# The order of work within an attention round: maximum products, values and relative products dealt out anew

## The chip, the cores and the metric

The kernel is one launch on one core of a Trainium2 chip. It computes one whole transformer layer. The metric is the device time in microseconds (us) of that launch. The engines are named PE (TensorE, matrix products), DVE (VectorE), ACT (ScalarE), POOL (GpSimd) and SP (which only issues DMA transfers). Each engine runs its own list of instructions in order, and they wait for one another by semaphores.

## The reference

Everything is float32, batch 2, sequence 2048, width 256, 16 heads of 16, relative positions clipped at 64.

```
x = x + attention(layernorm(x));  x = x + ffn(layernorm(x))

q, k, v = split(x @ W_qkv + b_qkv);  q = q / sqrt(16)
score = q . k  +  q . pe_k[clip(j - i, -64, 64) + 64]
attn  = softmax(score)
ctx   = attn @ v  +  sum_j attn[i, j] * pe_v[clip(j - i, -64, 64) + 64]
out   = ctx @ W_out + b_out

ffn: fp4_linear(silu(fp4_linear(x, w_gate)) * fp4_linear(x, w_up), w_down)
     (fp4: both operands rounded in blocks of 16 to a grid of 8 magnitudes)
```

## The kernel before, in words

The program has three parts, one after the other: `projections` (layer norm, Q, K, V), `attention`, and `ffn`. The change is in `attention` alone.

**Rounds.** Attention runs in 32 rounds. A round is one block of 512 queries of one group of four heads (2 batches x 4 groups x 4 blocks). The keys of a batch (2048) are walked in 16 steps, so a round has 16 steps, and each step has four half units: two tiles' worth of scores, 128 keys by 512 queries each, called **S** here. PE computes the scores transposed (keys in the partitions) into one of four PSUM banks `psS`, and ACT takes the exponential out of the bank. Steps 0 and 1 are the band near the diagonal (`near_half`, lines 916 and 923: four transposes that add the relative scores, then four products). Steps 2 to 15 are far from it (`far_half`, line 934).

**The maximum comes first.** The exponential needs the maximum of each row, and it is found one round ahead. For that PE computes the same scores once more, queries in the partitions, 64 products of 128 x 512 a round. Such a **maximum product** (**M** in the tables, line 826) goes to one of three PSUM banks `psA`, and DVE reduces it to one column (line 1115, `take`). The three banks go round: product number j waits until DVE has read product number j - 3 (`slot_free`). Three more things use that ring of banks, once a round each: the turned context (**D**, line 864), the denominators turned back (**B**, line 873), and the relative value products (**P**, line 959).

**The other letters.** **V** is the values of a step (line 848, `far_values`): probabilities times V, accumulated in the bank `psC`; a step's V is issued in the step after it, and in step 2 the letter stands for the band's values (line 946). **R** is the relative products (line 836): q times the table of relative keys, for the next round, into two banks of `psS`, from which ACT copies them to `rel_scores` (line 1061) and DVE later takes their maximum (`rel_maxima`, line 1120). There are four R in a round. After the last of them a DMA writes `rel_scores` to DRAM and two DMAs read it back skewed as `rel_near` for the next round. **T** (line 856) turns the negated maxima, and **F** (line 971) adds the relative values to `psC`. In steps 7 to 12 of the middle rounds, DVE also does one small operation a step on the weights of the FFN (lines 1207 to 1234).

**What sets the order.** The order is written out by hand: `ORDER` has one word of letters per step. PE goes through a word and issues what each letter says. DVE goes through the same words and does what concerns it, in the same order. ACT goes through its units in order. `RATE` counts the M of each step. The M of steps 13 to 15 (`AHEAD`) belong already to the round after the next, since the next round's maxima are made final at the start of step 13. `place`, `rel_place` and `half_at` number the half units and the relative products in the one sequence of `psS` banks. `RSTEP = 4` says that the four R stand at the end of steps 4 to 7.

## Time and profile before

| | |
|---|---|
| median of 3 runs | 2372.92 us (2371.45 to 2374.48) |
| profiled execution | 2376.86 us |
| its span, from first to last instruction | 2375.1 us |
| PE busy / DVE busy / ACT busy | 2254.8 / 1884.2 / 1431.0 us |
| attention's 32 rounds | from 173.9 us to about 1970 us of the span |
| mean granted TensorE clock | 0.976 of full speed |

A busy PE in this profile is not a PE at its peak: a product's record lasts 0.38 us, while the next one starts 0.22 us after it, so the records overlap and short waits hide under them. What PE really loses is read from the starts: where two successive products start further apart than the same pair does elsewhere, PE has waited.

### The profile page before, as it was taken

To read this page: it belongs to the slowest core of one execution; us is meant where nothing else is said; L and a number is where in the kernel's file an instruction comes from. 1 tells how busy PE (TensorE), PEld (TensorE's weight loads), DVE (VectorE), ACT (ScalarE), POOL (GpSimd) and SP (SyncE) were. 2 spreads that over 40 slices of the span, in tenths; PEclk is the share of its full clock that TensorE was granted. 3 is DMA by queue.
4 is the path that set the end of the run, shared out by engine and by line. 5 is a ranking of instruction groups with operands and counts; after the bars stand their busy time and mean duration, and the time that the engine had idled before them with its cause. 6 is when DMAs were issued, how large, how long until landed. Compare 5 with 4: busy or idle time off the path is not lost. (4 is left out here: it accounts for less than half of the span.)

```text
span 2375.1 us, 53033 instructions
## 1 busy us (share of the span) xinstructions
PE 2254.8 (95%) x21292; PEld 1157.4 (49%) x21292; DVE 1884.2 (79%) x3617; ACT 1431.0 (60%) x2720; POOL 600.4 (25%) x355
## 2 busy tenths in 40 slices
PE   6989999999999999999999999999999997999997
PEld 3514444444444444444444444444444444666665
DVE  5787788888888788878887888878888725999997
ACT  3406666677776666666666666666777673444442
POOL 5502222333322222222222222323332220111111
PEclk9959999999999999999999999999999998999999
DMA  5733533332334234433332342333222221111110
GB/s 160 195 90 92 134 90 93 97 93 84 92 100 116 83 98 106 110 88 93 93 97 79 103 97 84 97 92 93 84 84 84 83 72 43 45 44 44 47 50 20
DMA packets 275682, 210.68 MB, mean 89 GB/s; under 512 B 17058, under 2 KB 266628, under 8 KB 275332
## 3 DMA queue, kind: packets, MB, share of 16 engines
q1 hardware_dynamic: 274308, 203.37, 31.2%
q0 software_dynamic: 1152, 4.19, 0.6%
q8 instruction: 159, 2.61, 0.5%
q14 instruction: 63, 0.52, 0.1%
HBM read 113.35 MB, written 93.34 MB: 87 GB/s over the span
## 5 line engine op out<-in xcount | busy, mean ns | idle before, releaser
L1115 DVE TENSOR_REDUCE amax<-psA 128x1 f32<-128x512 f32 x2048 | 1300.8, 683 | 271.6 <-PE psA L826 267.2
L1082 ACT ACTIVATE probs<-psS 128x512 f32<-128x512 f32 x1792 | 928.7, 610 | 372.1 <-PE psS L934 370.2
L826 PE MATMUL psA<-keys,queries 96*128 96x512 bf16 x2048 | 782.0, 392 | 23.1 <-DVE amax L1115 17.9
L934 PE MATMUL psS<-queries,keys 102*128 102x512 bf16 (+7 forms) x2176 | 642.7, 343 | 2.1 <-issue 2.0
L848 PE MATMUL psC<-probs,vals 128*32 128x512 f32 (+7 forms) x4352 | 481.0, 528 | 4.2 <-issue 3.7
L784 POOL TENSOR_TENSOR band_probs<-band_probs,side 128x2048 f32<-128x2048 f32 x64 | 289.0, 4537 | 506.8 <-PE psC L946 506.8
L826 PEld LDWEIGHTS psA<-keys,queries 96*128 96x128 bf16 x2048 | 197.2, 98 | 444.2 <-DVE amax L1115 316.0
L934 PEld LDWEIGHTS psS<-queries,keys 102*128 102x128 bf16 (+1 forms) x2176 | 208.0, 98 | 186.2 <-ACT rel_scores L1061 18.1
L1077 ACT ACTIVATE band_probs<-psS 128x512 f32<-128x512 f32 x256 | 153.0, 598 | 159.6 <-PE psS L923 159.5
L848 PEld LDWEIGHTS psC<-probs,vals 128*32 128x32 f32 (+1 forms) x4352 | 89.4, 102 | 197.0 <-ACT probs L1082 128.5
L1438 PE MATMUL psG<-w_gate_up_T,f_xqT 128*128 128x352 f32 x512 | 160.4, 467 | 0.9 <-ACT f_xqT L1492 0.9
L1061 ACT COPY rel_scores<-psS 128x512 f32<-128x512 f32 x256 | 137.2, 590 | 31.1 <-PE psS L836 30.7
L916 PE MATMUL psS<-ident,rel_near 128*128 128x128 f32 x1024 | 155.5, 274 | 0.0
L790 POOL TENSOR_TENSOR band_probs<-band_probs 128x2048 f32<-128x2048 f32 x32 | 145.2, 4538 | 6.0 <-POOL band_probs L788 3.2
L916 PEld LDWEIGHTS psS<-ident,rel_near 128*128 128x128 f32 x1024 | 129.1, 142 | 23.6 <-issue 0.9
L1377 POOL TENSOR_TENSOR f_hq<-f_h_grid,f_h_scale 128x704 f32<-128x704 f32 x32 | 44.4, 1387 | 375.0 <-DVE f_h_grid L1606 375.0
L1438 PEld LDWEIGHTS psG<-w_gate_up_T,f_xqT 128*128 128x128 f32 x512 | 96.5, 193 | 50.5 <-issue 3.0
L770 POOL CAST shift<-shift_res 32x128 bf16<-32x128 f32 x32 | 9.0, 281 | 423.4 <-ACT shift_res L1050 423.4
L923 PE MATMUL psS<-queries,keys 102*128 102x128 bf16 (+1 forms) x1024 | 100.2, 220 | 4.9 <-DMA queries<-shift 4.9
L764 POOL MEMSET rel_near<- 128x256 f32 x16 | 5.1, 317 | 380.5 <-DMA rel_near<-rel_skew 380.5
L1470 PE MATMUL psD<-w_down_T,f_hqT 128*128 128x256 f32 (+1 forms) x384 | 96.2, 393 | 2.0 <-ACT f_hqT L1498 2.0
L1492 ACT COPY f_xqT<-psH 128x256 f32<-128x256 f32 x32 | 11.9, 373 | 129.1 <-PE psH L1429 129.1
(161 smaller groups left out, 2017.3 us busy)
## 6 DMA issues: line engine op xcount, KB each, us to landing
rel_skew<-rel_scores SPq DMA_DIRECT2D x32, 2048.0 KB, 9.2
rel_near<-rel_skew SPq DMA_DIRECT2D x64, 1024.0 KB, 8.2
keys<-k_ring SPq DMA_DIRECT2D x48, 256.0 KB, 5.8
queries<-q_parts SPq DMA_DIRECT2D x192, 64.0 KB, 2.4
ctx_d<-rden SPq DMA_DIRECT2D x32, 256.0 KB, 2.3
ctx_in<-ctx_d SPq DMA_DIRECT2D x32, 256.0 KB, 2.7
q_parts<-parts SPq DMA_DIRECT2D x16, 384.0 KB, 3.0
k_ring<-parts SPq DMA_DIRECT2D x12, 384.0 KB, 3.1
```

The source lines that it names most:

```text
L784: p.tensor_mul(both, both, c.side[:, e, None, :].broadcast_to([P, APAIRS, P])).then_inc(side_cut, 1)
L790: p.tensor_add(band[:, 0].rearrange("p h u q -> p (h u q)"), band[:, 0].rearrange("p h u q -> p (h u q)"), band[:, 1].rearrange("p h u q - ...
L826: t.matmul(small("M", m, n), qs[0:NR, qb, h, u * P:(u + 1) * P], keys[0:NR, par, h, c0:c0 + NQ], start=True, stop=True).then_inc(small_rea ...
L848: ins = t.matmul(psC[32 * h:32 * h + v.shape[1], q0:q0 + k], v, probs[:, n % 4, h % 2, o:o + k], start=False, stop=False, skip_group_check ...
L916: t.matmul(bank[:, u * P:(u + 1) * P], near[:, h * CH + u, e, :], c.ident[:], start=(u == 0), stop=False, is_transpose=True, skip_group_ch ...
L923: ins = t.matmul(bank[:, u * P:(u + 1) * P], keys[0:nr, par, h, c0:c0 + P], qs[0:nr, qb, h, u * P:(u + 1) * P], start=False, stop=(u == CH ...
L934: ins = t.matmul(bank[:, o:o + k], keys[0:nr, par, h, c0:c0 + P], qs[0:nr, qb, h, q0:q0 + k], start=True, stop=True, skip_group_check=True)
L1061: a.copy(rel[:, x:x + 2, :].rearrange("p x r -> p (x r)"), psS[:, j % SBANKS, :]).then_inc(unit_done, 1)
L1077: ins = a.activation(band[:, e, 2 * c2 + half].rearrange("p u q -> p (u q)"), src, ACT.Exp)
L1082: ins = a.activation(probs[:, n % 4, half], src, ACT.Exp)
L1115: v.reduce_max(amax[:, pair, k:k + 1], small("M", m, n), AX.X).then_inc(small_taken, 1)
L1438: ins = t.matmul(psG[:, half, 0:GU], xqT[:, k, cc, :], wgu[:, cc, half * GU:(half + 1) * GU], start=(cc == 0), stop=(cc == 1))
```

## The change

The words of `ORDER` are written anew. A round still has 64 M, 64 S, 14 V and the band's values, 4 R, and one each of D, B, P, F and T. What changes is where they stand:

- The M of the 16 steps were 7 6 5 4 3 3 3 4 4 4 5 4 3 3 3 3. They are now 9 4 5 4 6 1 3 4 5 2 4 5 0 4 5 3. The last three steps have 12 instead of 9, so 12 products (before: 9) are done ahead of the first round.
- V stood near the end of its step, behind the fourth S in most steps. It now stands in mid-step, mostly behind the second or third S.
- The four R stood at the end of steps 4, 5, 6 and 7. They now stand in steps 0, 1, 4 and 6.
- The maximum of the relative products had no letter: it stood behind the third M of the step after its R. It now has the letter **X**, in steps 1, 2, 5 and 7.

```diff
-RSTEP = 4
 RUNITS = APAIRS // 4
 SEQ = UNITS + RUNITS
+RSTEPS = (0, 1, 4, 6)
 ORDER = (
-    "SMSMVMSMSMMM", "SMSMMSDMSMM", "SMSMMVBSMSM", "SMSMSMSVM",
-    "SMSSMSVRM", "SMSSMSVRM", "SMSSMSVRM", "SMSMSMSVRM",
-    "SMSMSMSVPM", "SMSMSMSVM", "SMSMSMSMVFM", "SMSMSMSVM",
-    "SMSSMSVM", "SMSSMSVMT", "SMSSMSVM", "SMSSMSVM",
+    "SMMSMVMMMSMSRMM", "SMSMXSMSMDR", "MSSMXMVBSMMS", "SSMSMVMSM",
+    "SMSSMSMVMMRM", "SSMXSVS", "MSMSSSMVR", "MSMMXSVSMS",
+    "MSSMSMVPMSM", "SSMSVMS", "SSMSMMVFMS", "MSMSVSMSMM",
+    "SSSVS", "SMSSMSMVMT", "MSMVMSMSMS", "MSSSMVMS",
 )
...
-    return n if ends else n + min(max(n // 2 - RSTEP, 0), RUNITS)
+    return n if ends else n + sum(r < n // 2 for r in RSTEPS)
...
-    return 2 * (RSTEP + k) + 2 + k
+    return 2 * RSTEPS[k] + 2 + k
...
-                                rel_products(it + 1, qb1, step - RSTEP)
+                                rel_products(it + 1, qb1, RSTEPS.index(step))
...
-                    if n % 2 == 1 and RSTEP <= n // 2 < RSTEP + RUNITS and not ends:
-                        copy_rel(it + 1, n // 2 - RSTEP)
+                    if n % 2 == 1 and n // 2 in RSTEPS and not ends:
+                        copy_rel(it + 1, RSTEPS.index(n // 2))
...
-                    k = 0
                     for kind in ORDER[step]:
                         if kind == "M":
                             if todo:
                                 take(*todo.pop(0))
-                            k += 1
-                            if RSTEP < step <= RSTEP + RUNITS and k == 3 and not ends:
-                                rel_maxima(it + 1, step - RSTEP - 1)
+                        elif kind == "X" and not ends:
+                            rel_maxima(it + 1, RSTEPS.index(step - 1))
```

Three places show what moves. The first is PE in the second round, from the last products of step 1 to the band's values in step 2 (`psA` is the ring of the maximum products, `psS` holds scores or relative products, `psC` the values). Before:

```order
L916 MATMUL psS<-ident,rel_near 128x128 x4
L923 MATMUL psS<-queries,keys 128x128 x4
L826 MATMUL psA<-keys,queries 128x512 x2
L934 MATMUL psS<-queries,keys 128x384
L934 MATMUL psS<-queries,keys 128x128
L826 MATMUL psA<-keys,queries 128x512
L934 MATMUL psS<-queries,keys 128x384
L934 MATMUL psS<-queries,keys 128x128
L826 MATMUL psA<-keys,queries 128x512 x2
L946 MATMUL psC<-band_probs,vals 32x128 x4
```

And now, from the last maximum product of step 1 on:

```order
L826 MATMUL psA<-keys,queries 128x512
L864 MATMUL psA<-ident,ctx_sum 128x128 x4
L836 MATMUL psS<-rel_rows,queries 128x256 x4
L826 MATMUL psA<-keys,queries 128x512
L934 MATMUL psS<-queries,keys 128x384
L934 MATMUL psS<-queries,keys 128x128
L934 MATMUL psS<-queries,keys 128x384
L934 MATMUL psS<-queries,keys 128x128
L826 MATMUL psA<-keys,queries 128x512 x2
L946 MATMUL psC<-band_probs,vals 32x128 x4
```

Between the last near half of step 1 and the band's values there were five maximum products; now there are three, and the relative products and the turned context stand among them.

The second place is PE from the end of step 7 (the products behind the relative products or behind the third S) to the relative value products in step 8. Before:

```order
L836 MATMUL psS<-rel_rows,queries 128x256 x4
L826 MATMUL psA<-keys,queries 128x512
L934 MATMUL psS<-queries,keys 128x512
L826 MATMUL psA<-keys,queries 128x512
L934 MATMUL psS<-queries,keys 128x512
L826 MATMUL psA<-keys,queries 128x512
L934 MATMUL psS<-queries,keys 128x512
L826 MATMUL psA<-keys,queries 128x512
L934 MATMUL psS<-queries,keys 128x512
L848 MATMUL psC<-probs,vals 32x512 x4
L959 MATMUL psA<-band_probs,tv 32x32 x64
```

And now:

```order
L848 MATMUL psC<-probs,vals 32x512 x4
L934 MATMUL psS<-queries,keys 128x512
L826 MATMUL psA<-keys,queries 128x512
L934 MATMUL psS<-queries,keys 128x512
L826 MATMUL psA<-keys,queries 128x512
L934 MATMUL psS<-queries,keys 128x512 x2
L826 MATMUL psA<-keys,queries 128x512
L934 MATMUL psS<-queries,keys 128x512
L826 MATMUL psA<-keys,queries 128x512
L848 MATMUL psC<-probs,vals 32x512 x4
L959 MATMUL psA<-band_probs,tv 32x32 x64
```

The strict alternation of M and S is broken by a pair of S, and the V of step 7 stands before the last two S of that step instead of behind them.

The third place is DVE in a round of the middle, from step 6 to step 10 (`amax` is the maximum of one product, `rel_max_of` that of relative products, the `w_` tiles are the FFN's weights). Before:

```order
L1115 TENSOR_REDUCE amax<-psA 128x1 x3
L1120 TENSOR_REDUCE rel_max_of<-rel_scores 128x4
L1115 TENSOR_REDUCE amax<-psA 128x1
L1210 TENSOR_SCALAR w_scale<-w_scale 128x16
L1115 TENSOR_REDUCE amax<-psA 128x1 x3
L1120 TENSOR_REDUCE rel_max_of<-rel_scores 128x4
L1155 TENSOR_TENSOR rel_products<-psA,mask_q 128x16x16x2
L1115 TENSOR_REDUCE amax<-psA 128x1
L1213 RECIPROCAL w_scale<-w_scale 128x16
L1115 TENSOR_REDUCE amax<-psA 128x1 x4
L1216 TENSOR_SCALAR w_scale<-w_scale 128x16
L1115 TENSOR_REDUCE amax<-psA 128x1 x5
```

And now (the line numbers of the new kernel are two higher here, except those of the weights):

```order
L1117 TENSOR_REDUCE amax<-psA 128x1 x3
L1122 TENSOR_REDUCE rel_max_of<-rel_scores 128x4
L1117 TENSOR_REDUCE amax<-psA 128x1
L1210 TENSOR_SCALAR w_scale<-w_scale 128x16
L1117 TENSOR_REDUCE amax<-psA 128x1 x3
L1157 TENSOR_TENSOR rel_products<-psA,mask_q 128x16x16x2
L1117 TENSOR_REDUCE amax<-psA 128x1 x2
L1213 RECIPROCAL w_scale<-w_scale 128x16
L1117 TENSOR_REDUCE amax<-psA 128x1 x2
L1216 TENSOR_SCALAR w_scale<-w_scale 128x16
L1117 TENSOR_REDUCE amax<-psA 128x1 x4
```

One maximum of relative products has left step 8, and the M of the steps 9 and 10 have become fewer.

## Rows read from the trace of the kernel before

**Rows 1.** The page: busy times, and 40 slices with PE's share and granted clock.
```profile
PE 2254.8 (95%) x21292; PEld 1157.4 (49%) x21292; DVE 1884.2 (79%) x3617; ACT 1431.0 (60%) x2720; POOL 600.4 (25%) x355
...
PE   6989999999999999999999999999999997999997
...
PEclk9959999999999999999999999999999998999999
```

**Rows 2.** Windows of an undisturbed, a disturbed and the last-but-one round; columns in line one.
```profile
core 0: us, PE busy (x) PEld busy (x) DVE busy (x) ACT busy (x) POOL busy (x), PEclk, DMA share, GB/s
...
679.00:734.40 55.40, 55.03 (x611) 26.55 (x610) 45.49 (x80) 38.34 (x74) 14.96 (x7) 1.00 0.37 99
734.40:793.90 59.50, 56.37 (x611) 26.61 (x610) 45.78 (x80) 38.53 (x74) 15.29 (x8) 0.97 0.35 92
...
1866.80:1919.90 53.10, 52.89 (x602) 25.48 (x600) 39.27 (x66) 37.58 (x74) 15.23 (x8) 1.00 0.30 86
```

**Rows 3.** Timeline of PE, step 2: start, duration, line, what, [idle before].
```profile
688.25 0.60 PE L826 MATMUL psA<-keys,queries 96*128 96x512 bf16 x2
...
689.12 0.38 PE L934 MATMUL psS<-queries,keys 99*128 99x384 bf16 x2
689.41 0.39 PE L826 MATMUL psA<-keys,queries 96*128 96x512 bf16 x1
690.01 0.39 PE L826 MATMUL psA<-keys,queries 96*128 96x512 bf16 x1 [0.21 <-DVE amax L1115]
```

**Rows 4.** Timeline of PE, end of step 8 of the same round.
```profile
710.06 0.38 PE L826 MATMUL psA<-keys,queries 96*128 96x512 bf16 x1
710.28 0.38 PE L934 MATMUL psS<-queries,keys 102*128 102x512 bf16 x1
710.75 0.39 PE L826 MATMUL psA<-keys,queries 96*128 96x512 bf16 x1
710.97 0.38 PE L934 MATMUL psS<-queries,keys 102*128 102x512 bf16 x1
711.28 1.06 PE L848 MATMUL psC<-probs,vals 128*32 128x512 f32 x8
712.16 1.40 PE L959 MATMUL psA<-band_probs,tv 128*32 128x32 f32 x128
713.50 0.39 PE L826 MATMUL psA<-keys,queries 96*128 96x512 bf16 x1
```

**Rows 5.** Timeline of DVE, steps 2 and 8 to 9 of that round.
```profile
688.66 3.08 DVE L1115 TENSOR_REDUCE amax<-psA 128x1 f32<-128x512 f32 x5 [0.19 <-PE psA L826]
...
709.41 0.68 DVE L1120 TENSOR_REDUCE rel_max_of<-rel_scores 128x4 f32<-128x512 f32 x1
710.01 0.68 DVE L1115 TENSOR_REDUCE amax<-psA 128x1 f32<-128x512 f32 x1
710.61 0.16 DVE L1216 TENSOR_SCALAR w_scale<-w_scale 128x16 f32<-128x16 f32 x1
710.68 1.88 DVE L1115 TENSOR_REDUCE amax<-psA 128x1 f32<-128x512 f32 x3
...
714.84 0.42 DVE L1219 TENSOR_TENSOR w_tmp<-w_rows,w_scale 128x256 f32<-128x256 f32 x1
715.17 2.48 DVE L1115 TENSOR_REDUCE amax<-psA 128x1 f32<-128x512 f32 x4
```

**Rows 6.** Timeline of ACT, steps 6 and 7 of that round.
```profile
705.94 1.07 ACT L1061 COPY rel_scores<-psS 128x512 f32<-128x512 f32 x2
706.90 2.08 ACT L1082 ACTIVATE probs<-psS 128x512 f32<-128x512 f32 x4
```

**Rows 7.** Timeline of PE in the disturbed round, first product after the gap.
```profile
773.19 0.39 PE L826 MATMUL psA<-keys,queries 96*128 96x512 bf16 x1 [2.60 <-issue]
```

**Rows 8.** All waits of the span: engine, line, waited for: total us, times, longest.
```profile
PEld psA L826 <- DVE amax L1115: 316.0, 584, 2.1
```

**Rows 9.** Timeline of DVE ahead of the first round.
```profile
130.67 38.35 DVE L1115 TENSOR_REDUCE amax<-psA 128x1 f32<-128x512 f32 x64
...
169.59 5.47 DVE L1115 TENSOR_REDUCE amax<-psA 128x1 f32<-128x512 f32 x9
```

More of the change, by code:

```diff
@@ L1000, in iteration @@
                                 turn_maxima(it + 1)
+                        elif kind != "V":
+                            continue
                         elif step == 0:
```

## The prediction, written before the changed kernel ran

> **What bounds the kernel now.** I read the page first, then windows of single rounds, then the timelines of PE, DVE and ACT within one round. The page puts PE at 95% of the span with DVE at 79% behind it, and PE's share is 9 tenths or more in nearly every slice of attention [rows 1]. That is not yet a proof, since PE's records overlap. The windows show the size of a round: 55.40 us undisturbed, with DVE busy for 45.49 and ACT for 38.34 of them, and the clock at its full 2.4 GHz [rows 2]. So DVE and ACT each have 10 us or more to spare, and the round is PE's own work plus what PE waits for.
>
> How much it waits is in the starts. A maximum product (M) and a score half (S) follow each other at 0.22 us (710.06, 710.28) [rows 4]. In step 2 one M starts 0.60 us after the one before it (689.41, 690.01) and an earlier one 0.29 after its S [rows 3]. At the end of step 8 one starts 0.47 us behind its S (710.28, 710.75) [rows 4]. Against the 0.22 expected, that is 0.38, 0.07 and 0.25 us lost. I read the same six places (two in step 2, one each in steps 3, 8, 9 and 10) in the 29 rounds that begin between 233.0 and 1808.4 us. In the 23 undisturbed ones they sum to 1.16 to 1.73 us, mean 1.40; the round without them is 54.0 to 54.4 us, mean 54.2. In six rounds in which PE has a gap of 1.5 to 3.9 us with nothing to wait for, like the one of 2.60 us [rows 7], they sum to 1.09: DVE catches up during the gap. No other place of the round loses over 0.05 us on average.
>
> All six are M waiting for a bank that DVE has not yet emptied; that pair leads the waits of PE's loads, 584 times [rows 8].
>
> **The rule of these waits, from rows.** DVE starts on a product 0.41 us after PE starts it (688.25, 688.66), and then takes one each 0.60 us: five in 3.08, the last of 0.68 [rows 3, 5]. PE may start the product three later some 0.07 us after DVE is done: the second of those five begins at 689.26, ends at 689.94, and PE starts at 690.01. So product j can start 0.41 + 0.68 + 0.07 = 1.16 us after the start of product j-3, if DVE had no backlog. M and S in strict turns put four M into 1.31 us: the fourth has 0.15 us to spare, and each further one 0.16 less, because DVE needs 0.60 where PE brings one each 0.44. The fifth is on time by a hair; the sixth is late. Whatever else DVE does there adds to it: a maximum of relative products 0.60 (709.41 to 710.01), a weight operation 0.07 to 0.33 (710.61 to 710.68; 714.84 to 715.17) [rows 5], a mean of 0.24 over its ten kinds.
>
> **Step by step, before.** PE's time of a step (0.22 for M and S, 0.66 for a near S, 1.00 and 0.09 more for V, 0.45 for R, 1.33 for P, as their starts show) against DVE's: steps 7 to 11 take PE 3.27, 4.03, 2.82, 3.91, 2.82 us and DVE 3.23, 3.84, 2.64, 3.24, 2.64. For five steps DVE has next to no slack, so what it owes after step 7 comes due at the last M of steps 8, 9 and 10. In step 2 five M stand within 1.4 us behind an already full DVE. The same account puts the last M of step 8 at 0.40 late, those of step 9 at 0.21 and step 10 at 0.42, and those of step 2 at 0.45 in all; read: 0.44, 0.15, 0.27 and 0.46. It is good to about 0.15.
>
> **The change part by part.** No product, exponential or reduction is added or removed, so the 54.2 us stay and only waits can move.
>
> *The M dealt out anew.* PE's and DVE's time of the 16 steps, in us: 6.13/5.40, 4.41/3.16, 4.81/4.20, 2.82/2.40, 3.71/3.60, 2.17/1.19, 3.05/1.80, 2.82/3.23, 4.25/3.84, 2.39/1.44, 3.69/2.64, 3.04/3.24, 1.95/0.24, 2.94/3.07, 3.04/3.00, 2.61/1.80. Where DVE has more (7, 11, 13) the step before or behind has 1 us or more to spare (6, 12, 15), and the three banks carry the excess. I went through every M with the rule above. No product comes late. The least to spare is 0.15 us, at the fourth of four M in strict turns (into step 15), then 0.16 in step 0 and 0.18 to 0.20 once each in steps 2, 3 and 4. With each weight operation at 0.33 instead of 0.24, still none is late. So the six waits go: 1.40 us of a round.
>
> *V in mid-step.* It is the wait that this change could add: V of a step needs all four exponentials of that step, and it now stands two or three S into the next instead of four. ACT takes one each 0.49 us (four in 2.08) and a relative copy likewise [rows 6]; a bank is full 0.42 us after its S starts and the exponential lasts 0.60, so V can start 1.08 us after the last S of its step if ACT has no backlog. Before, V had 0.9 us or more to spare everywhere. Now it is 0.10 in step 11 (M S M S V behind the last S), 0.23 in step 15, 0.28 in step 12, 0.32 in steps 3 and 9, 0.49 and 0.54 in 8 and 10, more elsewhere. None late: cost 0. Queued behind a late V would be the next S and M, thus both other engines. V waiting for ACT doesn't occur in this trace; the bounds are 0 and what the second rival works out.
>
> *R in steps 0, 1, 4, 6.* 0.45 us on PE and 0.97 on ACT each, wherever they stand. Steps 0 and 1 are where ACT is idle most, since a near half takes PE 0.66 us plus its M. The banks that they take are free in time (least to spare 0.2 us, for an S in step 15). Their maxima (X) find the copy finished: the closest is step 2, where the copy ends 0.6 us before DVE gets there. The last R ends a step earlier, so the DMA out and back starts 3 us earlier and stays hidden. POOL's work on the band needs some 14 us between steps 2 and 8, of which there are 19. T still stands in step 13; steps 14 and 15 behind it are 0.4 us longer, which helps the shift's way back.
>
> *Twelve products ahead instead of nine.* Before the first round they run at DVE's pace, 38.35 / 64 = 0.60 us [rows 9]: 1.8 us more. The last-but-one round has three fewer, at 0.22: 0.65 us less, of 53.10 [rows 2].
>
> **The sum.** 23 x 1.40 + 6 x 1.09 = 38.7; the first and the last-but-one round, with fewer operations on DVE, about 1 each: 2.0; less 1.8, plus 0.65: 39.6. I take 1 off for places that are free by less than 0.2 us only on average: 38.6. From the profiled execution, 2376.9 - 38.6 = 2338.3 us; that execution lies 3.9 above the median of the runs, so the median becomes 2334. The rest of the span (projections, FFN) doesn't change.
>
> **Two rules of the Trainium skill.** The round's clock is 1.00 in spite of its waits of up to 0.4 us, and 0.97 in a round with the 2.60 us gap [rows 2, 7]. The Trainium skill ("TensorE: Matmul & The Clock Gate", section on a second HAM failure mode) says that short idles from cycling through PSUM banks make the clock swing. The trace disagrees here: there is no swing to be won back. By that rule the six dips would go as well, and 0.03 of 59.5 us, six times, would be 11 us more.
>
> PE's loads are busy for 26.55 of 55.40 us, DVE for 45.49 [rows 2]. The Trainium skill ("Perfetto Trace Analysis", on identifying the most-contended engine) counts TensorE by its weight loads and takes the busiest engine as the bound, so DVE. This is the third rival below.
>
> **The rivals.** *Half comes back* (12%). The spared times of 0.15 to 0.2 us are about as small as the account's own error. If every place with under 0.2 is late by 0.1 on average, and the backlog carries on, some 0.7 us a round return: 31 x 0.7 = 22, so 2356 us. For it: the account was off by 0.15 in step 10. Against: there it called too much, not too little.
>
> *V waits for ACT* (4%), the side on which it gets slower. If ACT's end reaches a V later than the 0.06 us I used, the spared times run out one by one. At 0.7 us more, the seven V named above are late by 0.60, 0.47, 0.42, 0.38, 0.38, 0.21, 0.16: 2.6 us a round against 1.4 saved, so 30 x 1.2 = 36 slower, 2409 us. It decides from about 0.5 us on. Against: DVE's end reaches PE in 0.07.
>
> *DVE is the bound* (4%). Then a round is DVE's 45.49 us and its own waits, reordering brings none of it away, and it stays at 2373. Against: DVE idles for 9.9 us a round and PE never for more than 0.4.
>
> **How the numbers follow.** The forecast has 80%, its own range 2325 to 2342 (the account's error of 0.15 us at one or two places a round, and PE's six gaps, 1.5 to 3.9 us each, which may be one or two more or fewer). The low end below, 2322, adds some other small waits that vanish. The high end, 2352, takes in most of the first rival. A change within 0.2% (4.7 us, about what a measurement of this kernel can tell) is 4%, slower 4%, faster 92%.
>
> **What would show it.** Right: rounds of 54.0 to 54.4 us instead of 55.4, no M starting over 0.3 us behind its predecessor outside the gaps, the waits of PE's loads for DVE well under 316 us, a first round that starts 1.8 us later. Wrong: undisturbed rounds of 55 us and more; V starting later than 0.31 us behind its predecessor in steps 11, 12 and 15 with ACT named as releaser; or new late M in steps 4, 7, 8 or 15.

## The result, and the profile after

| | before | after |
|---|---|---|
| median | 2372.61 us (2371.45 to 2374.48, 4 runs) | 2345.88 us (2339.8 to 2347.76, 4 runs) |
| profiled execution, its span | 2376.86, 2375.1 us | 2346.05, 2344.3 us |
| attention's first round begins, its last begins | 173.9, 1919.9 us | 175.5, 1886.3 us |

The ratio is 0.9882, with a 95% interval of 0.9863 to 0.9901: faster by 27 us, 1.2%, where 38.6 were forecast. The time lies in the forecast's range, but above the likeliest case's own range (2325 to 2342).

The page after, the rows that answer to [rows 1]:

```profile
PE 2235.5 (95%) x21292; PEld 1168.8 (50%) x21292; DVE 1905.2 (81%) x3617; ACT 1435.7 (61%) x2720; POOL 600.7 (26%) x355
...
PE   6989999999999999999999999999999996999997
...
PEclk9959999999999999999999999999999998999998
```

DVE has the same 3617 instructions and is busy for 21 us more. So some operations now last longer: that is the first trace of what the forecast missed.

Windows of three rounds and of seven microseconds after, in the columns of [rows 2]: a usual round, one with a gap, the last-but-one, and the stretch around the gap.

```profile
675.33:729.42 54.09, 54.09 (x611) 26.86 (x609) 45.58 (x81) 38.46 (x74) 14.96 (x7) 1.00 0.38 101
729.42:790.12 60.70, 57.22 (x611) 27.15 (x609) 46.72 (x81) 38.79 (x74) 15.28 (x8) 0.94 0.34 91
...
1833.79:1886.26 52.47, 52.04 (x598) 25.55 (x597) 37.51 (x63) 38.00 (x74) 15.29 (x8) 1.00 0.30 87
...
764.00:771.00 7.00, 3.62 (x12) 0.64 (x12) 2.11 (x4) 1.99 (x4) 0.00 (x0) 0.71 0.53 149
```

The usual round fell from 55.40 to 54.09 us, as predicted. The one with the gap did not fall: 59.50 before, 60.70 now, with a clock of 0.94 instead of 0.97.

PE in step 2 after, the answer to [rows 3]:

```profile
686.10 0.60 PE L934 MATMUL psS<-queries,keys 99*128 99x384 bf16 x4
686.54 0.60 PE L826 MATMUL psA<-keys,queries 96*128 96x512 bf16 x2
687.07 1.96 PE L946 MATMUL psC<-band_probs,vals 128*32 128x128 f32 x64
```

The 0.60 us between two M is gone; they form one row of two at 0.22. The waits of PE's loads for DVE, the answer to [rows 8], fell by 126 us:

```profile
DVE amax L1117 <- PE psA L826: 201.7, 430, 4.6
PEld psA L826 <- DVE amax L1117: 190.0, 299, 2.3
```

**Where the 30.8 us of the span went.** The 23 shortest of the 29 middle rounds, called undisturbed here, give 23 x (55.58 - 54.26) = 30.3. The six longest, those with the larger gaps, give 4.4 (355.5 to 351.1), the last-but-one 0.6, the first nothing (59.05 to 59.15). Ahead of the first round 1.6 are lost, and 2.8 behind the start of the last one. Two things stand out. In 7 of the 23 rounds one M in step 8 still comes 0.38 to 0.69 us late, 0.15 in the mean over all 23; this is most of why their mean is 54.26 and not 54.1. And eight rounds have gaps of 0.5 to 3.5 us (14.8 in all), where six (13.6) had them before. They are not quite the same rounds: the 19th after the first had a gap of 3.85 us before and has 0.56 now (61.61 to 54.71 us), while the fifth had none and has 1.95 now (55.48 to 57.88).

### The profile page after: what moved, and what is told of

The parts are those of the page before. It is cut to its first block and busy times, and to the rows that moved or that the text cites. A ratio compares the mean times of both kernels' runs of the same rounds, so it can differ in the third digit from the quotient of the medians.

```text
span 2344.3 us, 53033 instructions
## 1 busy us (share of the span) xinstructions
PE 2235.5 (95%) x21292; PEld 1168.8 (50%) x21292; DVE 1905.2 (81%) x3617; ACT 1435.7 (61%) x2720; POOL 600.7 (26%) x355
## 3 DMA queue, kind: packets, MB, share of 16 engines
q1 hardware_dynamic: 274308, 203.37, 31.4%
## 5 line engine op out<-in xcount | busy, mean ns | idle before, releaser
L826 PE MATMUL psA<-keys,queries 96*128 96x512 bf16 x2048 | 747.9, 391 | 6.2 <-DVE amax L1117 5.6
L934 PE MATMUL psS<-queries,keys 102*128 102x512 bf16 (+7 forms) x2176 | 596.2, 344 | 7.4 <-issue 6.9
L826 PEld LDWEIGHTS psA<-keys,queries 96*128 96x128 bf16 x2048 | 191.7, 98 | 319.5 <-DVE amax L1117 190.0
L934 PEld LDWEIGHTS psS<-queries,keys 102*128 102x128 bf16 (+1 forms) x2176 | 202.6, 98 | 270.1 <-ACT probs L1084 100.0
L1122 DVE TENSOR_REDUCE rel_max_of<-rel_scores 128x4 f32<-128x512 f32 x128 | 86.3, 675 | 2.3 <-ACT rel_scores L1063 2.3
```

The costliest lines, as they stand in the source:

```text
L826: t.matmul(small("M", m, n), qs[0:NR, qb, h, u * P:(u + 1) * P], keys[0:NR, par, h, c0:c0 + NQ], start=True, stop=True).then_inc(small_rea ...
L934: ins = t.matmul(bank[:, o:o + k], keys[0:nr, par, h, c0:c0 + P], qs[0:nr, qb, h, q0:q0 + k], start=True, stop=True, skip_group_check=True)
```

## First question: why DVE got slower

The late M is released by DVE. POOL and DVE in the round that begins at 345.5 us, from step 6 to 8, with the late M of PE:

```profile
369.55 4.53 POOL L790 TENSOR_TENSOR band_probs<-band_probs 128x2048 f32<-128x2048 f32 x1 [0.48 <-POOL band_probs L788]
...
371.94 2.29 DVE L1225 TENSOR_SCALAR w_bits<-w_bits 128x256 f32<-128x256 f32 x1
...
374.15 1.87 DVE L1117 TENSOR_REDUCE amax<-psA 128x1 f32<-128x512 f32 x3
...
377.27 0.39 PE L826 MATMUL psA<-keys,queries 96*128 96x512 bf16 x1 [0.53 <-DVE amax L1117]
```

The same operations before:

```profile
369.60 4.52 POOL L790 TENSOR_TENSOR band_probs<-band_probs 128x2048 f32<-128x2048 f32 x1 [0.48 <-POOL band_probs L788]
...
374.42 0.28 DVE L1225 TENSOR_SCALAR w_bits<-w_bits 128x256 f32<-128x256 f32 x1
```

POOL's addition ends at 374.1 us in both. Before, the weight operation of step 7 began after it and took 0.28 us. Now step 7 comes 2.5 us sooner, the operation begins inside the addition, and it ends with it (374.23), 2.29 us long. What DVE owes by then comes due at the last M of step 8. That is a theory of a lock between the two engines; its rival is that the longer time is a thing of the new order itself, wherever the operation stands.

**e1_weights_later.** The weight operations start a step later, behind POOL's addition. All else is the changed kernel.

```diff
-WSTEPS = range(7, 13)
+WSTEPS = (8, 9, 10, 11, 12, 15)
```

> The changed kernel with the six weight operations of a round in steps 8, 9, 10, 11, 12 and 15 instead of 7 to 12; nothing else differs. In the changed kernel's trace the weight operation of step 7 took 1.3 to 2.3 us in 16 rounds (0.3 to 0.5 elsewhere), always one of the lines 1219, 1225 and 1231, always while POOL added the two bands (line 790) and until about the end of that addition; in 8 of 23 undisturbed rounds a maximum product in step 8 was then 0.4 to 0.7 us late. Theory A (DVE waits for POOL's addition): no weight operation over 0.6 us, no late product in step 8, every undisturbed round 54.0 to 54.1 us instead of a mean of 54.26, and 4 to 6 us off the whole: about 0.998 of the changed kernel, 0.986 of the kernel before. Theory B (those operations are long for another reason, such as what they read): the long ones stay, now in step 8, and the time stays within 2 us of the changed kernel.

Measured: 2335.85 us (2333.8 to 2337.15, 4 runs), ratio to before 0.9854 [0.9835, 0.9872]. All times of that line, as minimum, median and longest (ns), in the changed kernel and in this one:

```profile
L1225 DVE TENSOR_SCALAR w_bits<-w_bits x16: 282/308/2292, 371.9 to 1747.1; 128x256 f32<-128x256 f32 x12, 128x352 f32<-128x352 f32 x4
```

```profile
L1225 DVE TENSOR_SCALAR w_bits<-w_bits x16: 281/284/335, 374.9 to 1745.2; 128x256 f32<-128x256 f32 x12, 128x352 f32<-128x352 f32 x4
```

DVE's busy time is back at 1884.3 us, the late M of step 8 is gone from the undisturbed rounds, and such a round takes 54.15 us. The lock holds, the rival falls. The gain of 10 us is more than the 4 to 6 expected. The spans of the two profiled executions differ by 8.9 us: 2.6 in the 23 undisturbed rounds, 4.3 in the six longest, 1.0 in the first, 0.2 ahead of it and 0.8 behind the start of the last. The gaps are no shorter (15.4 us in eight rounds), but in three rounds with gaps the granted clock is higher (the fifth and the 29th after the first have 1.00 instead of 0.97, the tenth 0.97 instead of 0.94). That the place of the weight operations brings this is not shown.

**e2_weights_earlier.** The opposite: the operations in steps 3 to 8, all beside POOL's work on the band.

```diff
-WSTEPS = range(7, 13)
+WSTEPS = range(3, 9)
```

> The changed kernel with the six weight operations in steps 3 to 8 instead of 7 to 12, all but the last inside the time in which POOL works on the band. Theory A (lines 1219, 1225 and 1231 wait until POOL's running operation, of up to 4.5 us, ends): some 50 to 70 of these operations take 1 to 4.5 us, maximum products behind them are late by up to 3 us, and the whole is 30 to 90 us slower than the changed kernel. The lines 1207, 1210, 1213 and 1216 stay at 0.1 to 0.5 us. Theory B (their length has nothing to do with POOL): within 5 us of the changed kernel.

Measured: 2479.16 us (2 runs), ratio 1.0448 [1.0416, 1.0479]: 133 us over the changed kernel, worse than I had put it. POOL and DVE in its round at 469.5 us:

```profile
483.36 4.53 POOL L784 TENSOR_TENSOR band_probs<-band_probs,side 128x2048 f32<-128x2048 f32 x1 [17.05 <-PE psC L946]
...
485.89 2.29 DVE L1231 TENSOR_TENSOR w_tmp<-w_tmp,w_bits 128x256 f32<-128x256 f32 x1
```

And two lines over the whole execution:

```profile
L1219 DVE TENSOR_TENSOR w_tmp<-w_rows,w_scale x16: 415/1488/2390, 322.5 to 1821.1; 128x256 f32<-128x256 f32 x12, 128x352 f32<-128x352 f32 x4
```

```profile
L1216 DVE TENSOR_SCALAR w_scale<-w_scale x16: 165/168/3757, 318.5 to 1817.2; 128x16 f32<-128x16 f32 x12, 128x22 f32<-128x22 f32 x4
```

Another POOL instruction (line 784) does the same as line 790, and an operation of 16 columns that takes 0.17 us by itself took 3.76. I had expected lines 1210 and 1216 to stay below 0.5 us; that was wrong. Over the whole execution 59 weight operations of the forms TENSOR_SCALAR and TENSOR_TENSOR (lines 1210, 1216 to 1234) began while a POOL instruction ran that would outlast them. All 59 became long, and all ended 0.03 to 0.39 us behind the end of POOL's instruction. The reductions (line 1207, longest 0.51 us) and the reciprocals (line 1213, 0.28) never did, though 22 of them began in the same way. The maxima of M kept their pace too (0.68 us each). In this round the M behind the blocked operations came 1.4 us late in step 3 and 1.6 in step 4, and the granted clock was 0.97 here and 0.95 from 1550 to 1700 us. My bounds had put no price on the clock.

The Trainium skill ("SBUF — State Buffer", section on who interferes with whom) says that GpSimd and VectorE share one pair of ports as an exclusive lock: who starts first has it for the whole instruction, and only VectorE's forms with two SBUF inputs or in a two-port mode ask for it, never a reduction. The trace agrees that reductions never waited, and that the others waited for the rest of POOL's instruction, up to 3.76 us for one of 4.5. Whether a TENSOR_SCALAR ran in a two-port mode is not seen in any row here.

## Second question: which part of the change brings the time

**e3_R_only.** R in steps 0, 1, 4, 6 and X behind them; M and V as before.

```diff
+RSTEPS = (0, 1, 4, 6)
+    "SMSMVMSMSMMMR", "SMSMMXSDMSMMR", "SMSMMXVBSMSM", "SMSMSMSVM",
+    "SMSSMSVRM", "SMSSMSVXM", "SMSSMSVRM", "SMSMSMSVXM",
+    "SMSMSMSVPM", "SMSMSMSVM", "SMSMSMSMVFM", "SMSMSMSVM",
+    "SMSSMSVM", "SMSSMSVMT", "SMSSMSVM", "SMSSMSVM",
```

> The words of the kernel before, with only the relative products moved to steps 0, 1, 4 and 6 and their maxima (X) to steps 1, 2, 5 and 7. Theory A (a round is PE's own 54.0 us plus maximum products that are late, by the rule that product j starts 1.16 us or more behind product j-3 plus DVE's backlog): the late ones of step 2 shrink from 0.46 to about 0.15, steps 9 and 10 stay, step 8 stays or grows; round 55.0 to 55.2 us instead of 55.58, so about 14 us less than before, 2359. Rival C (the relative products' place is most of the gain, because ACT is freed in steps 4 to 7): round near 54.3, 2348 or less.

Measured: 2362.52 us (2359.42 to 2365.02, 10 runs), ratio 0.9961 [0.9948, 0.9973]. An R at the end of step 1 gives DVE time in step 2: the loss there falls from 0.46 to 0.08, while step 8 keeps 0.37, step 9 0.15 and step 10 0.27 us. The undisturbed round takes 55.15 us, as theory A had it, and the rival (54.3) falls.

**e4_V_only.** V behind the second or third S of its step; M and R as before.

```diff
+RSTEPS = (4, 5, 6, 7)
+    "SMSMVMSMSMMM", "SMSMMSDMSMM", "SMSMMVBSMSM", "SMSMVSMSM",
+    "SMSVSMSRM", "SMSVSMSRMX", "SMSVSMSRMX", "SMSMVSMXSRM",
+    "SMSMVSMXSPM", "SMSMVSMSM", "SMSMVFSMSMM", "SMSMVSMSM",
+    "SMSVSMSM", "SMSVSMSMT", "SMSVSMSM", "SMSVSMSM",
```

> The words of the kernel before, with only the values moved to mid-step (behind the second S, or behind the third product of the ring); relative products in steps 4 to 7, the counts of maximum products as before. Theory A: the pause of 1 us breaks the turns of maximum products, so the late ones of steps 3 and 10 go and those of step 8 become small, step 2 stays at 0.46; round 54.9 to 55.2, about 2358 us. Rival D (values in mid-step wait for ACT): values start up to 0.3 us later than 0.31 behind their predecessor, ACT named, and the round stays at 55.5 or above.

Measured: 2371.78 us (2363.82 to 2375.1, 10 runs), ratio 0.9995 [0.9981, 1.0009]: no change, against 2358 expected; the undisturbed round takes 55.4. No V waits for ACT, so the rival isn't the reason. Step 2 keeps its late M. The losses of steps 8 to 10 moved rather than vanished: 0.15 to 0.2 us in the mean at the S behind F in step 10, and 0.08 and 0.16 at two M of step 11. My account of this order was wrong: DVE's debt of steps 7 to 11 is not paid by moving V, only passed on.

**e5_M_only.** M dealt out anew by both engines' time, found by the same rule as the prediction's, but not the dealing of the change; V stays at the end of its step and R in steps 4 to 7.

```diff
+RSTEPS = (4, 5, 6, 7)
+    "SMMSMMVMMSMMSMM", "SMSMMSDMSM", "SMMSVMBSSMM", "SSMSSV",
+    "MSSSSMVR", "SMSSMSMMVRMMX", "SSSMMSVRMMX", "SMSSXSMVR",
+    "SMMSSXSVP", "SSMSMSMVMM", "SMSSMSVFM", "MSMSSSV",
+    "MMSSSSMMV", "MSSSSMMMVT", "MSMSSMSMV", "MSMSSSMVMM",
```

> Values behind the last S of each step and relative products in steps 4 to 7 as before; only the maximum products (and the X in the step in which they were) are placed anew, 10 5 5 1 2 6 4 2 2 5 3 2 4 4 4 5 a step, so that by the rule none is late. Theory A: round 54.0 to 54.3 us, as good as the changed kernel within 0.2 us a round: 2340 to 2350 us. It would say that the new places of values and relative products are not needed for the gain. Rival E (all three parts are needed together): round 54.8 or more, 2362 or more.

Measured: 2332.41 us (2327.62 to 2340.02, 4 runs), ratio 0.9853 [0.9828, 0.9877]. A new dealing of M alone beats the whole change by 13 us, although its undisturbed round is longer (54.54 against 54.26, and 54.0 to 54.3 expected: S waits up to 0.08 us at three places of steps 5 and 8). What the change's own dealing of M gives alone was not run. The round that begins tenth after the first, next to the one behind it, in the columns of [rows 2]:

```profile
725.48:780.56 55.08, 54.60 (x610) 26.48 (x609) 45.99 (x81) 38.53 (x74) 15.29 (x8) 1.00 0.38 100
780.56:834.96 54.40, 54.40 (x611) 26.46 (x610) 46.39 (x81) 38.40 (x74) 15.73 (x9) 1.00 0.32 91
```

That is the round that takes 59.50 before and 60.70 after; here it takes 55.08. Its idle time of 0.48 us is the one gap that is left over all rounds. So the gaps are not a given of the program: something in the order makes them.

**e7_V_earlier.** In the changed kernel, V one S earlier in steps 3, 9, 11, 12 and 15. This measures the one hand-over that the prediction had from no row, ACT to V.

```diff
-SSMSMVMSM   SSMSVMS   MSMSVSMSMM   SSSVS   MSSSMVMS
+SSMVSMMSM   SSVMSMS   MSVMSSMSMM   SSVSS   MSSVSMMS
```

> The changed kernel with the values one or two letters earlier in the five steps where they had least to spare (3, 9, 11, 12, 15), so that by the account V is ready before the last exponential of its step: by 0.33 us in step 11, about 0.2 in 12 and 15, about 0.1 in 3 and 9. It measures what the trace of before did not show, a V that waits for ACT. Theory A (V starts 1.08 us after the last S of its step, 0.06 us after the exponential's end): V late by these amounts, some maximum products in steps 4 and 8 late as well, round 55.0 to 55.3, about 2375 us. Rival H (ACT's end reaches V much later than 0.06 us): V late by 0.5 us and more in each of the five, round over 56, 2400 us or more.

Measured: 2380.31 us (2376.33 to 2383.21, 10 runs), ratio 1.0029 [1.0016, 1.0042]. V is late by 0.10, 0.10, 0.32, 0.21 and 0.21 us in the five steps, all within about 0.01 of what an end of ACT that reaches PE 0.06 us later gives. The undisturbed round takes 55.36 us (55.0 to 55.3 expected). PE in step 11:

```profile
724.00 0.38 PE L934 MATMUL psS<-queries,keys 102*128 102x512 bf16 x1
724.63 1.06 PE L848 MATMUL psC<-probs,vals 128*32 128x512 f32 x8 [0.25 <-ACT probs L1084]
```

0.63 us instead of 0.31. In the changed kernel no V is late, so this step of the prediction was right, and the second rival's condition (ACT's end reaching V 0.5 us later) is excluded.

**e8_four_A_banks.** The order of before with four banks for M and three for S: the way to take the M waits away without any order.

```diff
-SBANKS, ABANKS = 4, 3
+SBANKS, ABANKS = 3, 4
```

> The order of the kernel before, unchanged, with four banks for the maximum products and three for the scores instead of three and four. It takes away what makes the maximum products wait: product j then waits for j-4. Theory A (the 1.4 us a round are these waits, and nothing else): no maximum product is late, score halves in steps 5 and 6 are late by 0.2 us each instead, rounds 54.4 to 54.8 us instead of 55.58, the whole 2340 to 2352. Against it (three score banks cost as much as they give): rounds of 55.4 and more, with waits of score halves for ACT's exponentials, 2370 or more.

Measured: 2363.48 us (2358.91 to 2367.65, 8 runs), ratio 0.996 [0.9945, 0.9975], against 2340 to 2352 expected. No M is late, but S is now: 0.27 us in each of steps 5 and 6, and 0.05 at many places of steps 5 to 8, behind ACT. Loads of PE for scores and what they wait for:

```profile
PEld psS L934 <- ACT probs L1084: 105.1, 272, 0.9
...
PEld psS L934 <- ACT rel_scores L1063: 92.7, 248, 0.6
```

The undisturbed round takes 55.28 us, between theory A (54.4 to 54.8) and what stood against it (55.4 and more). One bank moved turns most of one wait into another.

## Third question: where the gaps come from

PE and SP in the changed kernel's round of 60.70 us. SP's first row starts the write of the relative scores, its second the copy back:

```profile
763.51 0.38 PE L826 MATMUL psA<-keys,queries 96*128 96x512 bf16 x1
767.38 1.04 PE L934 MATMUL psS<-queries,keys 99*128 99x512 bf16 x2 [3.48 <-issue]
768.20 0.63 PE L826 MATMUL psA<-keys,queries 96*128 96x512 bf16 x1
768.63 0.63 PE L934 MATMUL psS<-queries,keys 99*128 99x512 bf16 x1
769.20 1.94 PE L848 MATMUL psC<-probs,vals 128*32 128x512 f32 x8
```

```profile
757.80 0.38 SPq L700 DMA_DIRECT2D rel_skew<-rel_scores  x1
767.21 2.05 SPq L703 DMA_DIRECT2D rel_near<-rel_skew  x2
```

PE waits for no engine ("issue"). The DMA queues of the same stretch, from the write's issue to its end and in the microsecond behind it:

```profile
DMA packets 2059, 2.09 MB, mean 291 GB/s; under 512 B 15, under 2 KB 2059, under 8 KB 2059
...
q1 hardware_dynamic: 2059, 2.09, 86.3%
...
DMA packets 3, 0.02 MB, mean 18 GB/s; under 512 B 0, under 2 KB 2, under 8 KB 2
...
q8 instruction: 1, 0.02, 5.5%
```

From 757.8 to 765 us there is only the write, on all 16 engines. The queue of PE's instructions has its packet at 765.07, behind the write, and PE goes on at 767.38, 2.3 us later. Before it is alike: packet at 770.88, in the midst of the write that was issued at 765.73, and the product after the gap at 773.19 [rows 7], 2.3 us later too.

The same two rows before, the write's issue and the packet (queue 8 from 770.5 to 771.5 us):

```profile
765.73 0.38 SPq L700 DMA_DIRECT2D rel_skew<-rel_scores  x1
```

```profile
q8 instruction: 1, 0.02, 5.5%
```

I read this as PE running out of instructions when their transfer stands behind or within the core's own write. The trace supports it in one more way. A packet of queue 8 has 16384 bytes. PE has 1225 recorded instructions (matrix products, weight loads and a few waits) in every middle round of both kernels. I divided the number of those ahead of the product that ends a gap by 256. The rest is 193 or 194 in all 14 gaps over 0.45 us, six before and eight after. In all 14 that product starts 2.2 to 2.4 us after the start of a packet of queue 8. So a gap always lies at the boundary of a block of 256 instructions, whatever product stands there. It also shows why only about every fifth round has a gap: five rounds are 6125 instructions, 19 short of 24 blocks, so after five rounds the boundary is back at nearly the same place of the round.

The change issues the write 3 us earlier (28.4 instead of 31.4 us into the round), since R is earlier, while the products near the gap come forward by only 1 (the relative value products from 33.4 to 32.3). I tested whether the write makes the gap by moving the write alone. The rival is that the gap belongs to the order of PE's instructions, whatever the DMA does.

**e9_skew_held.** The weights of e1; the write waits for a half unit of step 8 rather than for the last relative products.

```diff
-WSTEPS = range(7, 13)
+WSTEPS = (8, 9, 10, 11, 12, 15)
-halves_done(rel_half(m, RUNITS - 1) + 1)
+halves_done(half_at(m - 1, place(17), 0) if m
+            else rel_half(m, RUNITS - 1) + 1)
```

> The changed kernel with the weight operations in steps 8 to 12 and 15, and with the write of the skewed scores to DRAM held back about 2.4 us a round (until the third exponential of step 8; issue at about 30.8 us into the round instead of 28.4). Theory F (PE's gaps of 1.3 to 3.9 us are its instruction fetch standing behind the packets of that write: in the changed kernel the fetch that follows the relative value products starts at 35.6 to 35.9 us of the round, just when the write's packets end, and where the write starts at 32.3 and the products stand at 32.5 the fetch starts at 32.4 to 34.2 and there is hardly a gap): in rounds 1, 10, 15, 24 and 29 the fetch starts near 32 to 34 us, at most one or two gaps over 0.5 us remain, all but two of 29 rounds take 54.0 to 54.2 us, and 10 to 15 us go against the same kernel without the hold (2336): 2321 to 2327. Rival G (the gap belongs to the place in the program, whatever the DMA does): gaps in rounds 1, 5, 10, 15, 24, 29 stay, time within 3 us of 2336.

Measured: 2337.62 us (2335.57 to 2339.72, 4 runs), ratio 0.9852 [0.9828, 0.9877]: as long as e1, not the 2321 to 2327 expected. The write is issued at 32.4 us of most rounds, later than the 30.8 I had planned. There is no gap over 0.45 us in any round, with PE's instructions in the same order, so the rival falls. But the copy back now ends at 50.5 to 55.2 us of the round (45.8 to 49.0 in the changed kernel), and the next round's near scores wait for a transfer:

```profile
PE psS L923 <- DMA queries<-shift: 21.9, 15, 3.6
```

**e10_before_skew_held.** The same on the kernel before.

```diff
-halves_done(rel_half(m, RUNITS - 1) + 1)
+halves_done(half_at(m - 1, place(17), 1) if m
+            else rel_half(m, RUNITS - 1) + 1)
```

> The kernel before, unchanged but for the same write held back about 1.8 us (until the fourth exponential of step 8; issue at about 33.2 us instead of 31.4), so that it starts about when the relative value products end. The maximum products that are late stay as they are. Theory F: most of the six gaps go, undisturbed rounds stay at 55.6, and the whole takes 12 to 18 us less, 2355 to 2361. Rival G: six gaps, 2370 to 2376. If the copy back then lands too late for the next round, PE waits for a DMA at the start of rounds, and the whole gets slower than that.

Measured: 2368.6 us (2364.39 to 2370.8, 10 runs), ratio 0.998 [0.9967, 0.9993]. One gap of 1.31 us is left of six, but PE waits 12.7 us for the shift's transfer: some 5 us of the 12 to 18 expected. An undisturbed round keeps its length (55.53 us), so what the change took from those rounds is no matter of the DMA.

**e11_skew_held_less.** As e9, one place earlier: issued at 31.4 to 31.5 us of the round.

```diff
+halves_done(half_at(m - 1, place(16), 0) if m
+            else rel_half(m, RUNITS - 1) + 1)
```

> The changed kernel with the weight operations in steps 8 to 12 and 15, and the write of the skewed scores held back by only 1 to 3 us (until the first exponential of step 8, near 31.4 us of the round; 28.4 without a hold, 32.4 in the hold tried before). Theory I (the hold freed PE's instruction fetch, but the copy back then ended near 51.4 us of the round, with the shift's small transfers behind it in the queue, for which PE waited 15 times and 21.9 us at the start of a round): here the copy back ends near 50 us, that wait is 5 to 12 us in all, the gaps of PE are at most one or two over 0.5 us, and the whole takes 2324 to 2332 us, 5 to 12 less than with the longer hold. If both collisions shrink only in exchange for one another, 2335 to 2338.

Measured: 2324.95 us (2323.89 to 2328.19, 5 runs), ratio 0.9792 [0.9774, 0.981]: 11 us better than e1, within what was expected. Of the gaps one idle time of 0.53 us is left, and the wait for the shift halved (11.0 us, 10 times). The write starts where it starts in the kernel before, but PE's instructions are fetched at 32.0 instead of 36.5 us of this round, just ahead of it.

**e6_R_back.** The changed kernel's M and V with R in steps 4 to 7: the order's own way to a later write.

```diff
+RSTEPS = (4, 5, 6, 7)
+    "SMMSMVMMMSMSMM", "SMSMSMSMD", "MSSMMVBSMMS", "SSMSMVMSM",
+    "SMSSMSMVMMRM", "SSMXSVSR", "MSMSSSXMVR", "MSMMXSVSMSR",
+    "MSSMSMVPMXSM", "SSMSVMS", "SSMSMMVFMS", "MSMSVSMSMM",
```

> The changed kernel with the relative products back at the end of steps 4 to 7, their maxima in steps 5 to 8, and the values and nearly all maximum products where the change puts them. Theory A: one score half in step 6 late by 0.3 us (ACT has both exponentials and copies there), one maximum product in step 10 late by 0.1; undisturbed rounds 54.3 to 54.6 us against 54.26 with the relative products moved. The write starts at 31.4 us again, so fewer gaps of PE than in the changed kernel are possible; the whole 2338 to 2350 us. Rival C (the place of the relative products is most of the gain): rounds of 55 us or more, 2360 or more.

Measured: 2335.23 us (2334.66 to 2337.09, 4 runs), ratio 0.9837 [0.9816, 0.9859]. An undisturbed round is longer (54.55: one S in step 6 is 0.28 late). Yet of the gaps one idle time of 0.70 us is left, and the sum is 11 us better than the change. Beside the new places of M and V, moving R cost more than it brought; in e3, without them, it brought 10 us.

**e12_shift_first.** As e11, and POOL cuts the shift before it zeroes the band's edge.

```diff
+                cut_shift(it)
                 if qb in EDGES:
                     zero_edge(it, qb)
-                cut_shift(it)
```

> The kernel of the shorter hold (weight operations in steps 8 to 12 and 15, write held until the first exponential of step 8), with one more change: on POOL the cut of the shift now stands ahead of the zeroing of the skewed scores' edge, not behind it. In the kernel of the shorter hold the shift's transfers are issued 1.1 us after the turned maxima (49.4 us of the round) in rounds without an edge, but at 51 to 54 us in the 14 rounds with one, some 0.8 us after the copy back has landed, because POOL waits for that landing first. Theory J: all rounds issue the shift near 49.4 to 50, PE's wait for it at the start of rounds falls from 11.0 us (10 times) to the 3.6 to 4.5 us of the first round, and 5 to 8 us go: 2317 to 2321. If the shift's transfers wait in the DMA queue behind the copy back anyway, the wait stays and the time stays within 2 us of 2325.

Measured: 2314.19 us (2312.68 to 2318.74, 5 runs), ratio 0.9758 [0.9742, 0.9773]. This is the best kernel of the study, 32 us under the changed one and 58 under the one before; 2317 to 2321 were expected. The round that had the gap, and the usual one ahead of it:

```profile
720.57:775.32 54.75, 54.19 (x611) 26.65 (x609) 45.51 (x81) 38.58 (x74) 15.22 (x8) 1.00 0.38 100
666.49:720.57 54.08, 54.08 (x610) 26.86 (x609) 45.47 (x81) 38.46 (x74) 14.97 (x7) 1.00 0.39 101
```

Its DMA queues in the microsecond from 752.3 on, in which the write begins:

```profile
q1 hardware_dynamic: 92, 0.09, 26.0%
q8 instruction: 1, 0.02, 10.1%
```

PE's instructions come at 752.6 us, 0.4 us ahead of the write's first packets. What is left of the gap is 0.56 us of idle time ahead of one S. The profile puts it down to ACT, but I read it as the rest of the gap: the S stands at the boundary of a block (rest 194), and the same S is on time in all 28 other middle rounds.

```profile
754.66 0.38 PE L826 MATMUL psA<-keys,queries 96*128 96x512 bf16 x1
755.61 0.61 PE L934 MATMUL psS<-queries,keys 99*128 99x512 bf16 x2 [0.56 <-ACT probs L1084]
```

All 29 middle rounds take 54.15 us in the mean. PE's products wait for the shift's transfer only once more, 0.6 us in the first round, where it had been 3.6 even in the changed kernel. That round is 3.1 us shorter than there (56.06), but it begins 2.3 us later (177.85), so only 0.8 of it is gained.

## Why the prediction was right, and where it was not

**Right: what bounds the kernel.** The round is PE's starts plus its waits. By the third rival the time would have stayed at 2373; it didn't. DVE was even busy for 21 us more while the span fell by 31. (It had 9.9 us to spare in a round before, not the "10 us or more" of the prediction.)

**Right: the rule of the M waits.** The forecast had 1.40 us of each undisturbed round, 32.2 in all; 1.32 and 30.3 came. None of the M with 0.15 to 0.20 us to spare came late, so the first rival (small waits everywhere) has no trace either. e3 shows the rule at work in another order (55.15 us a round, 55.0 to 55.2 expected). In e5 the M were on time too, but the round was 0.24 us over its range by waits of S, which the rule does not have. In e4 it failed, by 14 us.

**Right: V waits for nobody**, with its hand-over confirmed by e7.

**Wrong: "with each weight operation at 0.33 instead of 0.24, still none is late".** I took their durations from where they stood and held them constant. But POOL's addition ends at 27.2 to 28.2 us of a round before and at 27.6 to 28.6 now, while step 7's operation moved from 28.5 to 26.5. Its length became 1.3 to 2.3 us in 16 rounds. So one of my own signs did not come true: in 7 of the 23 undisturbed rounds an M in step 8 starts more than 0.3 us behind its predecessor. A new late M in step 8 was also one of my signs of being wrong. It costs 0.15 us a round in the mean, 3.5 in the 23, more than the 1.9 us that these rounds gave less; with the operations moved (e1) they give 2.6 back.

**Wrong: R's DMA "starts 3 us earlier and stays hidden".** Data of the next round it is, and hidden for them. I named the consumer of the data and not who else uses the DMA engines. The six gaps I had kept as they were, give or take one or two; they depend on whether the write or PE's instructions come first. Against the forecast the rounds with gaps gave 2.1 us less. Against what was to be had it is more: e6 and e11 each put the write's place at some 11 us.

**Mis-sized.** The first and the last-but-one round gave 2.2 us less than I had put down without a row of their own; the gain of the first was nothing. Behind the start of the last round 2.8 us were lost, where I had said that nothing changes; that stretch takes 453 to 461 us over the kernels of this study without a pattern that I found, and stays open. Ahead of the first round it was 1.6 instead of 1.8. The terms together: 1.9 + 2.1 + 2.2 + 2.8 - 0.2, less the 1 that I had taken off, are the 7.8 us by which the profiled span missed. Further 3.7 us lie between the profiled execution and the median: I carried over that the one before was 3.9 above its median, and the one after was 0.2 above. The result of 2346 lies in the stated range by luck in part: its upper part was meant for the first rival, which did not occur, and none of these misses had a term in it except one or two gaps more.

**Why not every round has a gap.** In the twelfth round after the first the packet of PE's instructions comes at 35.9 us too, and PE has no gap: it reaches the next block's boundary only at 39.7 us of that round, 3.8 us behind the packet. In the tenth it would have reached it at about 34.3 us, and goes on at 38.0, 2.3 us behind the packet.

**Still open:** what a block's transfer waits for within the write, since the trace has the time of its packet and not of its request; and why gaps of the same length come with different granted clocks.

## What to carry to other kernels

When an order is changed, list for each engine what runs at the same time on the engines beside it, not only what it waits for: an operation that takes 0.3 us alone took 2.3 us beside POOL's addition, and the sum of busy time at a constant count shows it at once. A gap on the bounding engine that waits for nothing is to be held against the DMA queues, the instructions' own among them; here another 32 us, more than the 27 of the change itself, lay in moving one write by 3 us, the small operations by a step and one POOL call by one place. And try the parts of a change alone: here a new dealing of M alone was 13 us better than the whole change.

## What the runs showed of the hardware

- PE's instructions come in packets of 16384 bytes on a queue of their own, and a gap of PE that waits for nothing lay at a boundary of 256 of PE's recorded instructions every time (14 of 14 in the two kernels). In the changed kernel the packet came when the core's own write of 2 MB had ended (35.6 to 35.9 us of the round) in six of the seven rounds read, and PE went on 2.2 to 2.4 us after such a packet. In the best kernel, with the write later, it came at 32.0 us of the tenth round after the first.
- A gap can bring a lower granted clock, and then costs more. Around the gap of 3.48 us the clock was 0.71 in the mean from 764 to 771 us, and the eight products of a V took 1.94 us instead of 1.06. The rounds with the gaps of 3.48 and 3.39 us took 6 us more than a usual one, about twice the gap itself. A gap of 1.67 at a clock of 1.00 cost 2.7. Near 2 us both occur: in the 29th round after the first a gap of 1.91 came with 0.97 in the changed kernel, one of 2.06 with 1.00 in e1.
- Of DVE's small operations, those of form TENSOR_TENSOR and TENSOR_SCALAR that began within one of POOL's additions lasted until its end, even at 16 columns (3.76 us instead of 0.17); reductions and reciprocals did not.
- ACT's end reaches a waiting PE product in about 0.06 us (e7: an exponential ends at 724.58, V starts at 724.63), DVE's in 0.06 to 0.07 (before: 689.95 to 690.01).
